# Four-layer kernel on Trainium2, Mamba part: a third buffer for GpSimd's products, one fp32 matrix buffer, and two operations moved from GpSimd to VectorE

## The chip, the cores and the metric

One core of one Trainium2 chip runs the whole program in one launch. The metric is device time in microseconds (us), the median of repeated executions. The profile comes from one more execution under the hardware profiler. Engines: PE is TensorE, with PEld for its weight loads; DVE is VectorE; ACT is ScalarE; POOL is GpSimd; SP is SyncE, which issues most DMAs here.

## The reference, cut to what matters

The program computes four residual layers over a sequence of 4096 tokens of width 256: linear attention, a feed-forward layer, two Mamba blocks, and a mixture of experts. The change touches the Mamba blocks only. Their reference, for each of the two layers:

```
xz = x_norm @ in_w.T ; xb, z = split(xz)            # 512 channels each
xb = silu(causal_conv4(xb) + cb)
delta, Bm, Cm = split(xb @ xp_w.T)                  # 16, 16, 16 values per token
delta = softplus(delta @ dtw.T + dtb)               # per channel and token
dA = exp(delta[..., None] * -exp(a_log))            # per channel, token, state n of 16
mi = delta[..., None] * Bm * xb[..., None]
step t:  v = 0.6 * v + mi_t ; h = dA_t * h + v ; y_t = sum over n of h * C_t
out = ((y + dp * xb) * silu(z)) @ ow.T
```

## The kernel before, in words

**Tiling.** `mamba_phase` runs once per layer. A layer is 16 chunks of 256 tokens (`NCM`, `CM`). Channels lie on the partitions in four groups m of 128 (`KI`). A chunk has 16 slots, one for each state n. Two chunks make one turn of a hardware loop (`Fori`), except the first two and the last two on GpSimd and TensorE.

**One slot.** TensorE makes v (`velocity`, L1298 and L1300: 32 bf16 matmuls). ScalarE makes dA (`decays`, L1149). VectorE runs four scans for h (`scan`, L1019). GpSimd multiplies h by the row C of this state (`product`, L898), into the fp32 tile `hc`. TensorE adds `hc` over the states with an identity matrix (`accumulate`, L1282, in two halves). The scans lie in a ring of four buffers, `hc` in two: product k waits until product k-2 is added (`acc_done`), and also until the first scan of slot n+1 is done. TensorE adds product n-2 in slot n, behind the velocity matmuls of slot n+1, half by half.

**Work of other chunks in the slots.** A slot has two steps, `at` = 2n and 2n+1. Beside the slot's own work each engine runs `tail(...)`, which ends the chunk before (the gate with skip and y, L1002 on VectorE; times silu(z), L888 on GpSimd; output projection L1271; its sum into the residual, L1008 on VectorE), and `head(c+1, ..., at+10)`, which prepares the next chunk. The order on each engine is written out by hand by these step numbers, and every engine works its list in order.

**The steps of `head` that matter here**, by their number (the slot is that number less 10, halved):

- 21: GpSimd makes `Gf` (L866) and the first matrix `Mf[:, 0]` (L843), decay times B. There are two, for the two halves of 128 tokens. 23: the second one.
- 22 to 26: softplus. ScalarE: L1109, exp L1115, square L1118, exp L1122, logarithm L1125. VectorE: clamp L975 at 23, the series L979 at 26.
- 24 and 27: ScalarE rounds `Mf` to bf16, `Mhi` (L1130). 25 and 30: GpSimd makes the rest, `Mlo` (L849).
- 27: VectorE ends delta with L984 and two L986. GpSimd: `Glo`, the low part of the matrix of the carries (L876).
- 28: GpSimd makes `u` = delta times xb (L880). 30: TensorE transposes it (L1247). 31 to 35: bf16 parts (L1135, L992), carries, and the DMAs that place the parts for the next chunk.

**Loops and queues.** SP places the bf16 matrices when both halves of `Mhi`, and then of `Mlo`, are there; it spreads the rows of C two states at a time behind the products. Neither list is changed.

Of the kernel before, what the change touches and what calls it, by code (L numbers as in the profile page):

```python
# [14 lines left out]
ALU = mybir.AluOpType  # L15
# [649 lines left out]
def mamba_phase(net, layer, xm):  # L665
# [4 lines left out]
    with ExitStack() as ctx:  # L670
# [16 lines left out]
        Mf = sb("Mf", [P, TM, NS, SUB])  # L687
# [10 lines left out]
        hc = sb("hc", [P, 2, KI, CM])  # L698
# [20 lines left out]
        with nc.Block() as block:  # L719
            @block.sync  # L720
            def _(sp):
# [7 lines left out]
                for part in range(3):  # L729
                    at = SUB + part * NS  # L730
                    sp.dma_start(Mf[at:at + NS, 0], dram["decay"][SUB:SUB + NS]).then_inc(s["loaded"], 16)
                    sp.dma_start(Gf[at:at + NS, 0], dram["carry_on"]).then_inc(s["loaded"], 16)
# [96 lines left out]
            def _(pool):  # L829
# [11 lines left out]
                def matrix(q, j):  # L841
                    pool.wait_ge(s["b_done"], 1 + q + 1)
                    nc.gpsimd.tensor_tensor(Mf[:, j], decay_n, Bs[:, j, :].unsqueeze(2).broadcast_to([P, NS, SUB]),  # L843
                                            ALU.mult).then_inc(s["mf_done"], 1)

                def matrix_low(q, j):
                    pool.wait_ge(s["mhi_done"], 1 + q * TM + j + 1)
                    pool.wait_ge(s["m_moved"], 1 + 6 * 16 * q)
                    nc.gpsimd.tensor_tensor(Mlo[:, j], Mf[:, j], Mhi[:, j], ALU.subtract).then_inc(s["mlo_done"], 1)  # L849

                def head(q, par, at):
# [18 lines left out]
                    if at == 23:  # L870
                        matrix(q, 1)
                    if at == 25:
                        matrix_low(q, 0)
                    if at == 27:
                        pool.wait_ge(s["ghi_done"], 1 + q + 1)
                        nc.gpsimd.tensor_tensor(Glo[:], Gf[:].rearrange("p j i n -> p j (i n)"), Ghi[:],  # L876
                                                ALU.subtract).then_inc(s["glo_done"], 1)
                    if at == 28:
                        pool.wait_ge(s["delta_done"], 1 + q + 1)
                        nc.gpsimd.tensor_tensor(u[:], delta[:, par], xb[:, par], ALU.mult).then_inc(s["u_done"], 1)  # L880
# [9 lines left out]
                def product(c, par, n, next_scan=1):  # L890
# [3 lines left out]
                    pool.wait_ge(s["acc_done"], 1 + AHEAD + k - 1)  # L894
# [3 lines left out]
                    nc.gpsimd.tensor_tensor(hc[:, n % 2], h[:, n % RING],  # L898
# [32 lines left out]
            def _(dve):  # L931
# [3 lines left out]
                for par in range(2):  # L935
                    nc.vector.memset(U2[SUB:KV, par, 0], 0.0)
                    for j in range(NSUB):
                        nc.vector.tensor_copy(M2[SUB:SUB + 2 * NS, par, j], Mf[SUB:SUB + 2 * NS, 0])
                        nc.vector.tensor_copy(M2[SUB + 2 * NS:KV, par, j], Mf[SUB + 2 * NS:KV, 0])
# [4 lines left out]
                for par in range(2):  # L944
                    for j in range(NSUB):
                        nc.vector.tensor_tensor(M2[SUB + 2 * NS:KV, par, j], Mf[SUB + 2 * NS:KV, 0],
# [14 lines left out]
                def head(q, par, at):  # L961
# [19 lines left out]
                    if at == 27:  # L981
# [6 lines left out]
                        last.then_inc(s["delta_done"], 1)  # L988
                    if at == 32:
# [60 lines left out]
            def _(act):  # L1050
# [13 lines left out]
                def head(q, par, at):  # L1064
# [61 lines left out]
                    if at in (24, 27):  # L1126
# [1060 lines left out]
```

## Time and profile before

| | |
|---|---|
| runs | 4496.07, 4501.99, 4504.96 us; median 4501.99 us |
| profiled execution | 4487.59 us, span of the trace 4485.9 us |
| mean granted TensorE clock | 0.866 of full speed |
| busy over the span | PE 79%, DVE 62%, POOL 46%, ACT 44% |
| first Mamba layer, first to last scan | 1058.8 to 2296.7 us |
| second Mamba layer | 2410.9 to 3658.5 us |

Busy shares are means over the whole program. PE is the busiest engine, but a share doesn't tell which wait ends last in a slot: for that the timeline of one chunk is needed, engine by engine, with the idle time ahead of each instruction in brackets.

### The profile page before, as it was taken

Reading aid. Unit: us, or ns where it says so; the run is one execution under the profiler, and the core shown is the slowest. Engines: PE = TensorE matmul, PEld = TensorE weight load, DVE = VectorE, ACT = ScalarE, POOL = GpSimd, SP = SyncE. Lnnn points to the kernel's source line nnn. Section 1 sums busy time; section 2 is a strip of 40 time slices with the busy share of each in tenths; the row PEclk is TensorE's granted clock in tenths of the full one; section 3 lists DMA queues with packets and bytes.
Section 4 is the critical chain, followed back from the end, with each engine's and each line's share of the span. In section 5 each row is a group of like instructions: output and inputs, shape, how many; then the busy total and the mean of one; then the engine's idle time right before and its main releaser. Section 6 shows DMA issues by size and latency. Waiting matters only on the chain. (4 is left out here: it accounts for less than half of the span.)

```text
span 4485.9 us, 88366 instructions
## 1 busy us (share of the span) xinstructions
PE 3543.9 (79%) x28412; PEld 2364.3 (53%) x28413; DVE 2774.5 (62%) x4814; ACT 1980.0 (44%) x4446; POOL 2046.1 (46%) x1206
## 2 busy tenths in 40 slices
PE   6888869936898888888856988889888863199980
PEld 4554546614555555555534555555555543188870
DVE  3444432345777777777765777777777767255545
ACT  1212112215666565665625666566565633133320
POOL 0101000014666676666744667676676764500006
PEclk8888878967999999999987999999999985599995
DMA  4000000012223121231211212122121223311113
GB/s 143 0 0 0 0 21 0 0 56 55 59 53 76 49 74 52 52 74 48 74 38 45 69 50 73 51 60 66 51 73 51 62 74 106 141 47 47 49 37 109
DMA packets 152098, 244.93 MB, mean 55 GB/s; under 512 B 25714, under 2 KB 74130, under 8 KB 149012
## 3 DMA queue, kind: packets, MB, share of 16 engines
q1 hardware_dynamic: 142356, 212.69, 17.4%
q0 software_dynamic: 9344, 27.27, 1.8%
q8 instruction: 208, 3.41, 0.3%
q14 instruction: 190, 1.56, 0.1%
HBM read 119.89 MB, written 38.27 MB: 35 GB/s over the span
## 5 line engine op out<-in xcount | busy, mean ns | idle before, releaser
L898 POOL TENSOR_TENSOR m_hc<-m_h,m_Cb 128x1024 f32<-128x1024 f32 x512 | 1205.4, 2355 | 763.5 <-DVE m_h L1019 466.2
L1019 DVE TENSOR_TENSOR_SCAN m_h<-m_dA,m_hlast,m_bank 128x256 f32<-128x256 f32 x2048 | 1354.2, 725 | 140.1 <-PE m_bank L1300 74.0
L1282 PE MATMUL m_bank<-m_hc,ident 128*128 128x512 f32 x2048 | 1207.7, 679 | 148.5 <-POOL m_hc L898 148.3
L1149 ACT ACTIVATE m_dA<-m_delta,m_rate 128x256 f32<-128x256 f32 x2048 | 894.1, 500 | 16.4 <-DVE m_h L1019 15.4
L1298 PEld LDWEIGHTS m_bank<-m_M,m_U 128*128 128x128 bf16 x8192 | 605.0, 101 | 358.3 <-DVE m_h L1019 222.2
L1298 PE MATMUL m_bank<-m_M,m_U 128*128 128x64 bf16 x8192 | 674.9, 197 | 124.5 <-DVE m_h L1019 117.0
L1300 PEld LDWEIGHTS m_bank<-m_M,m_U 112*128 112x128 bf16 x8192 | 578.5, 100 | 204.5 <-issue 172.6
L1300 PE MATMUL m_bank<-m_M,m_U 112*128 112x64 bf16 x8192 | 675.2, 197 | 0.0
L1282 PEld LDWEIGHTS m_bank<-m_hc,ident 128*128 128x128 f32 x2048 | 337.3, 204 | 198.0 <-POOL m_hc L898 164.9
L967 DVE SCALAR_TENSOR_TENSOR m_cv<-m_xpre,m_conv,m_cv 128x256 f32<-128x256 f32 x384 | 273.3, 753 | 22.6 <-ACT m_cv L1087 18.1
L1212 PE MATMUL m_bank<-m_pair,m_in 128*128 128x256 f32 x1024 | 268.7, 389 | 8.2 <-ACT m_cv L1087 4.4
L1947 ACT ACTIVATE x_h<-x_bank,x_b 128x256 f32<-128x256 f32 x320 | 134.4, 471 | 284.9 <-PE x_bank L1893 277.3
L1212 PEld LDWEIGHTS m_bank<-m_pair,m_in 128*128 128x128 f32 x1024 | 194.6, 194 | 120.0 <-issue 93.9
L108 POOL TENSOR_SCALAR var_eps<-a_mv 128x4 f32<-128x4 f32 x16 | 3.7, 229 | 524.8 <-DVE a_mv L120 524.8
L1861 POOL DMA_DIRECT2D slots_y<-x_y x40 | 21.7, 542 | 445.7 <-DVE x_y L1988 445.7
L403 PE MATMUL a_bank<-a_qh,a_phi 128*128 128x512 f32 x256 | 144.5, 699 | 48.1 <-DVE a_qh L238 39.0
L1893 PE MATMUL x_bank<-x_xhi,r_wlo 128*128 128x256 bf16 x640 | 175.8, 275 | 6.0 <-issue 5.0
L1893 PE MATMUL x_bank<-x_xlo,r_whi 128*128 128x256 bf16 x640 | 175.6, 274 | 0.0
L1893 PE MATMUL x_bank<-x_xhi,r_whi 128*128 128x256 bf16 x640 | 175.5, 274 | 0.0
L1906 PE MATMUL x_bank<-r_whi,x_hhi 128*128 x640 | 174.4, 273 | 0.0
L1906 PE MATMUL x_bank<-r_whi,x_hlo 128*128 x640 | 174.4, 273 | 0.0
L1906 PE MATMUL x_bank<-r_wlo,x_hhi 128*128 x640 | 174.4, 273 | 0.0
(260 smaller groups left out, 5594.2 us busy)
## 6 DMA issues: line engine op xcount, KB each, us to landing
m_Cb<-m_c_rows SPq DMA_DIRECT2D x256, 256.0 KB, 3.2
m_M<-m_Mhi SPq DMA_DIRECT2D x128, 256.0 KB, 4.1
m_M<-m_Mlo SPq DMA_DIRECT2D x64, 256.0 KB, 3.9
m_U<-m_Uhi SPq DMA_DIRECT2D x128, 128.0 KB, 3.3
slots_x<-x_res SPq DMA_DIRECT2D x40, 256.0 KB, 3.0
x_x_in<-slots_x SPq DMA_DIRECT2D x40, 256.0 KB, 2.6
slots_y<-x_y POOLq DMA_DIRECT2D x40, 256.0 KB, 2.3
m_U<-m_Ulo SPq DMA_DIRECT2D x64, 128.0 KB, 3.6
```

The source lines that it names most:

```text
L403: nc.tensor.matmul(B[5 + g % 2][:].rearrange("p (h t) -> p h t", h=4), phi[:, KD + g // 2, t], qh[:, 4 * g:4 * g + 4, t], start=True, stop ...
L898: nc.gpsimd.tensor_tensor(hc[:, n % 2], h[:, n % RING], Cb[:, g % 2, n % NG, :].unsqueeze(1).broadcast_to([P, KI, CM]), ALU.mult).then_inc ...
L967: i = nc.vector.scalar_tensor_tensor(cv[:, m, :], xpre[:, m, k:k + CM], conv[:, m, k:k + 1], cv[:, m, :], ALU.mult, ALU.add)
L1019: nc.vector.tensor_tensor_scan(h[:, n % RING, m, :], dA[:, n % RING, m, :], VB[(n % 2) * 2 + g][:, (m % 2) * CM:(m % 2 + 1) * CM], hlast[: ...
L1149: nc.scalar.activation(dA[:, n % RING, m, :], delta[:, par, m, :], ACT.Exp, scale=rate[:, m, n:n + 1]).then_inc(s["da_done"], 1)
L1212: last = nc.tensor.matmul((H0, H1)[g % 2][:, m % 2 * CM:(m % 2 + 1) * CM], w_in[:, k, m * P:(m + 1) * P], xT[:, k, :], start=(k == 0), sto ...
L1282: last = nc.tensor.matmul(Y[half][:], net.ident[:], hc[:, n % 2, 2 * half:2 * half + 2, :], start=(n == 0), stop=(n == NS - 1))
L1298: nc.tensor.matmul(bank[:, at:at + SUB], U1[:, par, j, m * P:(m + 1) * P], M1[:, par, j, n, :], start=True, stop=False)
L1300: last = nc.tensor.matmul(bank[:, at:at + SUB], U2[:, par, j, m * P:(m + 1) * P], M2[:, par, j, n, :], start=False, stop=True)
L1893: last = nc.tensor.matmul(out, w_part[:, bass.ts(e * WB + kk * KH + m, P)], x_part[:, par, kk, :], start=(kk == 0 and n == 0), stop=(kk == ...
L1906: last = nc.tensor.matmul(YB[par][:, t * D:(t + 1) * D], h_part[:, par, m, t * P:(t + 1) * P], w_part[:, bass.ts(e * (WB // 2) + KD * KH / ...
L1947: last = nc.scalar.activation(h[:, g % 2, m % 2, :], HB[g][:, m % 2 * SLOT:(m % 2 + 1) * SLOT], ACT.Relu, bias=b1[:, bass.ts(e[par] * KH + ...
```

## The change

`hc` gets three buffers; product and accumulation take buffer (n + par) mod 3, where par is the chunk's parity. Product k then waits until product k-3 is added; across the chunks' border, where the numbers jump, two products keep the shorter distance. `Mf` has one buffer for both halves, so the second matrix is made behind `Mlo` of the first. `u` and `Glo` go to VectorE, `u` right behind delta, `Glo` at step 29. `Mhi` of the first half moves from 24 to 23 on ScalarE.

```diff
-        Mf = sb("Mf", [P, TM, NS, SUB])
+        Mf = sb("Mf", [P, NS, SUB])
-        hc = sb("hc", [P, 2, KI, CM])
+        hc = sb("hc", [P, 3, KI, CM])
...
                 def matrix(q, j):
                     pool.wait_ge(s["b_done"], 1 + q + 1)
+                    pool.wait_ge(s["mlo_done"], 1 + q * TM + j)
...
                         matrix(q, 0)
-                    if at == 23:
+                    if at == 24:
+                        matrix_low(q, 0)
+                    if at == 25:
+                        pool.wait_ge(s["mlo_done"], 1 + q * TM + 1)
                         matrix(q, 1)
-                    if at == 25:
-                        matrix_low(q, 0)
-                    if at == 27:
-                        pool.wait_ge(s["ghi_done"], 1 + q + 1)
-                        nc.gpsimd.tensor_tensor(Glo[:], Gf[:]..., Ghi[:], ALU.subtract)
-                    if at == 28:
-                        pool.wait_ge(s["delta_done"], 1 + q + 1)
-                        nc.gpsimd.tensor_tensor(u[:], delta[:, par], xb[:, par], ALU.mult)
                     if at == 30:
                         matrix_low(q, 1)
...
-                    pool.wait_ge(s["acc_done"], 1 + AHEAD + k - 1)
+                    pool.wait_ge(s["acc_done"], 1 + AHEAD + k - (1 if par == 0 and n < 2 else 2))
-                    nc.gpsimd.tensor_tensor(hc[:, n % 2], h[:, n % RING],
+                    nc.gpsimd.tensor_tensor(hc[:, (n + par) % 3], h[:, n % RING],
...
                         last.then_inc(s["delta_done"], 1)          # VectorE, step 27
+                        dve.wait_ge(s["delta_done"], 1 + q + 1)
+                        nc.vector.tensor_tensor(u[:], delta[:, par], xb[:, par], ALU.mult)
+                    if at == 29:
+                        dve.wait_ge(s["ghi_done"], 1 + q + 1)
+                        nc.vector.tensor_tensor(Glo[:], Gf[:]..., Ghi[:], ALU.subtract)
...
-                    if at in (24, 27):
-                        j = (at - 24) // 3
+                    if at in (23, 27):
+                        j = (at - 23) // 4
                         act.wait_ge(s["mf_done"], 1 + q * TM + j + 1)
-                        nc.scalar.copy(Mhi[:, j], Mf[:, j])
+                        nc.scalar.copy(Mhi[:, j], Mf[:])
```

The accumulation on TensorE takes its buffer by the same rule.

## Rows read from the trace of the kernel before

**Rows 1.** Windows: us; each engine's busy us (instructions); clock, DMA share, GB/s.
```profile
1058.80:2296.70 1237.90, 1095.04 (x10459) 687.32 (x10459) 952.96 (x1419) 768.32 (x1792) 842.82 (x418) 0.93 0.23 60
1824.50:1830.00 5.50, 5.18 (x27) 3.15 (x27) 4.20 (x8) 2.11 (x5) 5.50 (x3) 0.50 0.61 149
```

**Rows 2.** Waits, 1290 to 2168 (11 chunks): who for whom, us, times, longest.
```profile
PE m_bank L1282 <- POOL m_hc L898: 51.3, 33, 2.2
PE m_bank L1298 <- DVE m_h L1019: 40.4, 21, 2.7
PE m_bank L1247 <- POOL m_u L880: 8.3, 11, 1.3
...
POOL m_hc L898 <- PE m_bank L1282: 88.4, 56, 4.1
```

**Rows 3.** Timeline of VectorE, tenth chunk of layer 0: start, us, instruction, [idle before].
```profile
1808.76 3.93 DVE L1019 TENSOR_TENSOR_SCAN m_h<-m_dA,m_hlast,m_bank 128x256 f32<-128x256 f32 x6
1812.61 1.39 DVE L979 SCALAR_TENSOR_TENSOR m_pair<-m_pair,m_cv 128x1024 f32<-128x1024 f32 x1
...
1817.30 2.08 DVE L984 SCALAR_TENSOR_TENSOR m_u<-m_u,m_floor,m_pair 128x1024 f32<-128x1024 f32 x1 [2.01 <-ACT m_u L1125]
1819.41 1.29 DVE L986 TENSOR_TENSOR m_delta<-m_bank,m_u 128x512 f32<-128x512 f32 x2
1820.62 6.48 DVE L1019 TENSOR_TENSOR_SCAN m_h<-m_dA,m_hlast,m_bank 128x256 f32<-128x256 f32 x10
```

**Rows 4.** Timeline of GpSimd in the same stretch.
```profile
1808.69 1.90 POOL L843 TENSOR_TENSOR m_Mf<-m_decay,m_Bs 128x1024 f32<-128x1024 f32 x1
1810.55 2.37 POOL L898 TENSOR_TENSOR m_hc<-m_h,m_Cb 128x1024 f32<-128x1024 f32 x1
1812.87 3.11 POOL L849 TENSOR_TENSOR m_Mlo<-m_Mf,m_Mhi 128x1024 bf16<-128x1024 f32 x1
1815.95 2.34 POOL L898 TENSOR_TENSOR m_hc<-m_h,m_Cb 128x1024 f32<-128x1024 f32 x1
1818.25 1.41 POOL L876 TENSOR_TENSOR m_Glo<-m_Gf,m_Ghi 128x128 bf16<-128x128 f32 x1
1821.70 2.35 POOL L898 TENSOR_TENSOR m_hc<-m_h,m_Cb 128x1024 f32<-128x1024 f32 x1 [2.04 <-DVE m_h L1019]
1824.01 2.35 POOL L880 TENSOR_TENSOR m_u<-m_delta,m_xb 128x1024 f32<-128x1024 f32 x1
```

**Rows 5.** Timeline of ScalarE in the same stretch.
```profile
1811.21 1.04 ACT L1130 CAST m_Mhi<-m_Mf 128x1024 bf16<-128x1024 f32 x1
...
1816.21 1.06 ACT L1125 ACTIVATE m_u<-m_u 128x1024 f32<-128x1024 f32 x1
```

**Rows 6.** Timeline of TensorE in the same stretch.
```profile
1824.11 2.08 PE L1282 MATMUL m_bank<-m_hc,ident 128*128 128x512 f32 x2 [1.38 <-POOL m_hc L898]
1826.50 1.94 PE L1247 MATMUL m_bank<-ident,m_u 128*128 128x128 f32 x8 [0.32 <-POOL m_u L880]
```

**Rows 7.** One line each: count, shortest/median/longest ns, first and last start.
```profile
L984 DVE SCALAR_TENSOR_TENSOR m_u<-m_u,m_floor,m_pair x32: 1283/2078/2547, 1033.7 to 3575.4; 128x1024 f32<-128x1024 f32 x32
...
L849 POOL TENSOR_TENSOR m_Mlo<-m_Mf,m_Mhi x64: 2118/2190/3180, 1030.5 to 3586.4; 128x1024 bf16<-128x1024 f32 x64
...
L298 DVE TENSOR_TENSOR x_res<-x_res,a_zn x8: 1224/1225/1227, 112.9 to 647.4; 128x1024 f32 x7, 128x1024 f32<-128x1024 f32 x1
```

**Rows 8.** Timeline of VectorE and GpSimd at the start of that chunk.
```profile
1771.90 4.56 DVE L967 SCALAR_TENSOR_TENSOR m_cv<-m_xpre,m_conv,m_cv 128x256 f32<-128x256 f32 x6
1779.24 1.66 DVE L1002 SCALAR_TENSOR_TENSOR m_u<-m_xb,m_skip,m_bank 128x256 f32<-128x256 f32 x4 [0.20 <-PE m_bank L1282]
...
1771.60 2.36 POOL L898 TENSOR_TENSOR m_hc<-m_h,m_Cb 128x1024 f32<-128x1024 f32 x1 [2.23 <-PE m_bank L1282]
```

**Rows 9.** Timeline of VectorE and GpSimd at the end of layer 0.
```profile
2294.00 2.67 DVE L1019 TENSOR_TENSOR_SCAN m_h<-m_dA,m_hlast,m_bank 128x256 f32<-128x256 f32 x4 [0.23 <-PE m_bank L1300]
...
2296.35 4.64 POOL L898 TENSOR_TENSOR m_hc<-m_h,m_Cb 128x1024 f32<-128x1024 f32 x2 [0.53 <-PE m_bank L1282]
```

More of the change, by code:

```diff
@@ L848, in matrix_low @@
                     pool.wait_ge(s["m_moved"], 1 + 6 * 16 * q)
-                    nc.gpsimd.tensor_tensor(Mlo[:, j], Mf[:, j], Mhi[:, j], ALU.subtract).then_inc(s["mlo_done"], 1)
+                    nc.gpsimd.tensor_tensor(Mlo[:, j], Mf[:], Mhi[:, j], ALU.subtract).then_inc(s["mlo_done"], 1)
                 def head(q, par, at):
@@ L937, in _ @@
                     for j in range(NSUB):
[L938 to L939 removed]
+                        nc.vector.tensor_copy(M2[SUB:SUB + 2 * NS, par, j], Mf[SUB:SUB + 2 * NS])
+                        nc.vector.tensor_copy(M2[SUB + 2 * NS:KV, par, j], Mf[SUB + 2 * NS:KV])
                 on = Gf[:, 0].rearrange("p i n -> p (i n)")
@@ L988, in head @@
                         last.then_inc(s["delta_done"], 1)
+                        dve.wait_ge(s["delta_done"], 1 + q + 1)
+                        nc.vector.tensor_tensor(u[:], delta[:, par], xb[:, par], ALU.mult).then_inc(s["u_done"], 1)
+                    if at == 29:
+                        dve.wait_ge(s["ghi_done"], 1 + q + 1)
+                        nc.vector.tensor_tensor(Glo[:], Gf[:].rearrange("p j i n -> p j (i n)"), Ghi[:],
+                                                ALU.subtract).then_inc(s["glo_done"], 1)
                     if at == 32:
@@ L1274, in tail, with accumulate @@
                             last.then_inc(s["out_psum"], 1)
-                def accumulate(c, n, half):
+                def accumulate(c, par, n, half):
                     k = c * NS + n
@@ L1281, in accumulate @@
                         pe.wait_ge(s["gate_done"], 1 + c * KI + 2 * half + 2)
-                    last = nc.tensor.matmul(Y[half][:], net.ident[:], hc[:, n % 2, 2 * half:2 * half + 2, :],
+                    last = nc.tensor.matmul(Y[half][:], net.ident[:], hc[:, (n + par) % 3, 2 * half:2 * half + 2, :],
                                             start=(n == 0), stop=(n == NS - 1))
@@ L1302, in velocity, with late @@
                     last.then_inc(s["v_psum"], 1)
-                def late(c, n, half):
+                def late(c, par, n, half):
                     if not (isinstance(c, int) and c == 0):
-                        accumulate(c - 1, n + NS - 2, half)
+                        accumulate(c - 1, 1 - par, n + NS - 2, half)
                 def slots(c, par, more, more2):
@@ L1345, in _ @@
                 for n in range(2):
-                    late(NCM, n, 0)
-                    late(NCM, n, 1)
+                    late(NCM, 0, n, 0)
+                    late(NCM, 0, n, 1)
                 tail(NCM, 1, 7, False)
```

23 lines of the change are left out of this document (10 added, 13 removed).

## The prediction

> **What bounds the kernel now.** The change touches only the two Mamba layers, so I went from the page's shares to windows over one layer, then to the waits by pair, then to the timeline of one chunk, engine by engine. The window over the first layer lasts 1237.9 us; PE is busy in 1095.0 of them (88%), DVE in 953.0, POOL in 842.8 [rows 1]. For 16 chunks that is 77 us a chunk. No engine is full, but PE is close: its idle time is small and sits in a few places. The waits say which: over 11 chunks PE waits 51.3 us for GpSimd's products, 40.4 us for scans, 8.3 us for u [rows 2], so 9.1 us a chunk in the first two. GpSimd in turn waits 88.4 us, 8.0 a chunk, for the accumulations of the buffer that it wants to write [rows 2]; this is what a third buffer can remove. The reader is to ask of each of these waits whether something later depends on it.
>
> The timeline of a chunk answers. Of the 33 waits for products in 11 chunks three fall in each chunk, for products 1, 7 and 8 [rows 2]; from 1826.5 (slot 10) until the gate of the next chunk (L1002) PE has none. A product that comes earlier there finds PE with other work ahead of it. The gate itself waits 0.20 us for PE [rows 8], so PE also sets it. PE does wait in slots 8 to 10. There the order is: softplus on ScalarE ends at 1816.21 + 1.06 = 1817.27 [rows 5]; L984 on VectorE starts at 1817.30 but takes 2.08 us, where its shortest is 1.28 [rows 3, 7]. It ends at 1819.38, which is 1.09 after product 7 on GpSimd ended (1815.95 + 2.34 = 1818.29) [rows 4]. So L984, with two inputs in SBUF, did not run while the product ran. The same shows the other way round: the first Mlo takes 3.11 instead of its shortest 2.12 [rows 4, 7], being held until L979 ended at 1814.00; and L979 took 1.39 since it was held until product 6 ended at 1812.92, then needed 1.08. Behind L984 come two L986 (1.29), then scan 9 at 1820.62 [rows 3], product 8 at 1821.70 (1.08 after the scan's start), its addition on PE at 1824.11, and the transposes at 1826.50 [rows 4, 6]. This chain, ACT and POOL, then DVE, POOL, PE, sets the chunk's time.
>
> **The change part by part.**
>
> *One Mf buffer.* Before, the second Mf (1.90) filled the time ahead of product 6. Now product 6 follows product 5 and has to wait for the first scan of slot 7: 1808.76 + 1.08 (the same distance as at product 8) = 1809.84, so 0.71 earlier than 1810.55. It ends at 1812.2, and Mlo starts there; Mhi is ready, since ScalarE makes it one step earlier. L979 comes at 1812.61 [rows 3], finds Mlo running and is held until 1812.16 + 2.12 = 1814.28, then takes 1.08: 1815.36. The second Mf has to wait for Mlo's completion, so L979 gets in first; Mf then needs 1.90 less the 0.14 of its start that lies under the wait (the held Mlo ran 1.98 behind L979, against 2.12): 1817.12. Product 7 starts at 1817.1, where it started at 1815.95 [rows 4]. L984 still comes at 1817.30, because ScalarE's list has the same work in another order (Mhi's 1.04 moves ahead of the square, which then ends where Mhi ended, at 1812.25 at the latest [rows 5], still ahead of L979). Product 7 is 0.2 us ahead of L984. It runs to 1819.44, and L984 ends 1.08 later, at 1820.52, instead of 1819.38: **+1.14**.
>
> *u on VectorE.* It stands directly ahead of scan 9. Its price is that of a fp32 multiplication or addition of 1024 elements with both inputs in SBUF: L298, 1.225 us in all eight cases [rows 7]. Bounds: 1.08 (what L984 needs once it is let in) and 1.225 + 2.35, if a product is running in front of it. I take 1.225, less nothing, since after 1821.84 GpSimd is idle until scan 9. Scan 9 comes at 1820.62 + 1.14 + 1.24 = 1823.00: **+2.38**, and so do product 8 and its addition. What is saved is u on GpSimd (2.35), which was late for the transposes by 0.32 only [rows 6]: at 1824.11 + 2.38 the addition starts, 2.07 later the transposes, which wait for nothing now: 1828.57 against 1826.50. **+2.07 a chunk.** From there PE is full up to the gate, so it hands the delay on unchanged.
>
> *Glo on VectorE.* On GpSimd it took 1.41, nearly all of it held by L984 [rows 4]. On VectorE it stands behind scan 9's second half and has to wait until product 8 ends, at most 2.35. It must be there for the carries some 9 us later, and VectorE stands idle before L992 anyway. At nothing; if that cover goes, up to 0.9 for scan 10, between zero and that; I take zero.
>
> *The third buffer.* It removes most of the 8.0 us a chunk for which GpSimd waits for PE. None of the products that PE waits for (1, 7, 8) waits for an accumulation: they start behind scans or back to back. At nothing in 30 chunks; bounds -1.4 (below) and 0. At the end of a layer it counts: the last two products run back to back from 2296.35 [rows 9], and product 14 could have started at 2294.00 + 1.08 = 2295.1, so product 15 ends 1.3 us sooner: -1.3 for each layer, -2.6 in all. In each layer's first, unoverlapped head u costs 1.2 less, but the later Mf and Mlo stand in front of L984 and of u; I take zero, between -1.2 and +1.2.
>
> *TensorE's clock.* Behind its idle time PE runs at 0.50 of its clock, 1.2 GHz, from 1824.5 to 1830 [rows 1], and ahead of that it waited for products 7 and 8 and a scan [rows 2, 6]. The additions are at the low level there before and after; I add nothing. Idle time grows by 2 us, so if it falls sooner, an addition more is slow; it takes 2.08 at this level [rows 6], so +1 at the most.
>
> *Sum.* 15 chunks of 16 in each layer carry a head: 30 × 2.07 = +62, less 2.6: **+59 us**. On the profiled execution, 4487.6, that is 4547; on the median of the runs, 4502.0 (0.3% above the profiled one), 4561.
>
> A rule of the Trainium skill bears on the sum. The page "SBUF — State Buffer", section "SBUF: two separate sides", says that VectorE and GpSimd share one pair of ports as an exclusive lock, which a VectorE instruction with two SBUF inputs needs, and that the first to start keeps it to its end. The trace agrees for L984 and L979; no row of it shows a TENSOR_TENSOR of VectorE beside a GpSimd operation. If the pair were shared by bandwidth, the one Mf buffer would cost nothing and only u would count. The page "GPSIMD Engine Reference", section "Engine selection", advises VectorE for two-input elementwise work, as GpSimd takes about twice the time; the rows agree (2.35 against 1.225), and by that rule alone the change would gain, since it frees 2.35 + 1.41 of GpSimd for 1.4 of VectorE. I hold it for misleading here, because GpSimd's u lay beside PE's addition and VectorE's lies in the chain.
>
> **Rivals.**
>
> *B, L984 comes first.* The 0.2 us between product 7 and L984 is thin. If L984 is let in at 1817.30, it ends at 1818.58, L986 at 1819.9; product 7 ends at 1818.58 + 2.2 = 1820.8; u is held by it and ends 1.08 later, 1821.9. Scan 9 is then +1.2, the transposes +0.87: 30 × 0.87 - 2.6 = +23, 4525. For it: a delay of GpSimd's dispatch of 0.2. Against: back to back operations there show no gap [rows 4].
>
> *C, the delay is absorbed.* Somewhere between slot 10 and the next slot 8 a wait shrinks by what was added: no change, 4502. Against it: PE's list is full up to the gate, and from the gate on the chain runs through DVE, POOL and PE again.
>
> *D, faster.* The first convolution of a chunk (L967, six) takes 4.56 us, because product 15 holds it from 1771.90 to 1771.60 + 2.36 = 1773.96 [rows 8]: 2.06 lost, and with the third buffer product 15 is out of the way by then. If the gate depended on VectorE, this would come back; I take 1.5 as the mean of a chunk, between none and 2.06, so 45 us; with B's +23 that gives -22, 4480. It decides from the point where VectorE reaches the gate later than PE. Against: the gate waits for PE, by 0.20 even in this chunk [rows 8].
>
> *E, it doesn't do what it says.* A product still waits for its buffer, as the distance at the chunks' border stays short: it would take away the -2.6 only.
>
> **How the numbers follow.** Forecast (E with it) 0.55, own range 4549 to 4571 (the clock's and Glo's bounds above, the ends' below); B 0.23; C 0.10; D 0.12. The range holds forecast and B with what lies between and some above: 4508 to 4574. About 9 us, 0.2%, is what a measurement of this kernel can tell. Slower 0.55 + 0.23 = 0.78, same 0.10, faster 0.12.
>
> **What would show it.** Product 6 about 1.1 us behind the first scan of slot 7, L979 near 2.8 us long, product 7 starting ahead of L984, and L984 near 3.2 us long: the step of the one buffer. L984 near 1.3 and u near 2.2: B. u 1.2 us on VectorE and then scan 9: the second step. Products 12 to 15 without waits for PE, PE's waits unchanged: the third buffer off the path. Wrong would be transposes less than 18 us behind the first scan of slot 7 (17.7 before, 19.8 by the forecast, 18.6 by B), or a gate that no longer waits for PE.

## The result, and the profile after

| | before | after |
|---|---|---|
| median of 13 runs each, on the same chips | 4490.92 us (4480.94 to 4504.96) | 4525.75 us (4506.19 to 4536.18) |
| ratio | | 1.0078, 95% interval 1.0064 to 1.0091 |
| profiled execution | 4487.59 us, clock 0.866 | 4533.29 us, clock 0.864 |
| both Mamba layers, first to last scan | 2485.5 us | 2533.0 us |

Slower, as forecast, by 34.8 us (0.78%) where 59 (1.3%) was forecast. The forecast's base, 4502, was 11 us too high as well: it was a median of three runs. All the time is in the two Mamba layers, which are 47.5 us longer in the profiled executions. The whole profiled executions differ by 45.7 us; they lie 3 us below and 8 us above their medians, which makes up the difference to 34.8.

The windows over both layers (columns as in [rows 1]), after:

```profile
1059.51:2321.29 1261.78, 1101.07 (x10466) 695.15 (x10463) 996.27 (x1449) 769.30 (x1792) 787.01 (x388) 0.92 0.23 59
2435.20:3706.45 1271.25, 1108.55 (x10464) 698.92 (x10461) 997.10 (x1449) 768.90 (x1792) 786.87 (x388) 0.92 0.23 58
```

GpSimd is relieved: 787.0 us busy where it was 842.8 [rows 1]. VectorE has 43 more. TensorE does the same work and waits longer. The waits after, in the same stretch of time as in [rows 2], 10.8 chunks now:

```profile
POOL m_hc L893 <- DVE m_h L1020: 254.5, 102, 9.3
PE m_bank L1283 <- POOL m_hc L893: 63.5, 33, 3.3
PE m_bank L1299 <- DVE m_h L1020: 43.4, 22, 2.7
POOL m_hc L893 <- PE m_bank L1283: 40.9, 5, 8.2
```

GpSimd's waits for additions went from 56 to 5, and what it waits for now is scans. The five are product 0 of every second chunk, at the border where the distance stayed short. TensorE's waits for products are 33 as before, and grew from 51.3 to 63.5 [rows 2]: the third buffer removed waits for which nothing was late. The growth is at product 7, for which TensorE waits 3.26 us in the mean of a chunk and waited 2.18 before. The wait for u is gone.

The tenth chunk of layer 0 again, VectorE and then GpSimd, as [rows 3, 4]. The first scan of slot 7 is at 1820.83 (1808.76 before). Line numbers have shifted: the series is L974 here (L979 before), and the line with two inputs that ends softplus is L979 here (L984 before). That one is called "the last softplus step" below. The accumulation, L1283 here, is called the addition.

```profile
1820.83 3.93 DVE L1020 TENSOR_TENSOR_SCAN m_h<-m_dA,m_hlast,m_bank 128x256 f32<-128x256 f32 x6
1824.67 2.72 DVE L974 SCALAR_TENSOR_TENSOR m_pair<-m_pair,m_cv 128x1024 f32<-128x1024 f32 x1
...
1829.36 3.17 DVE L979 SCALAR_TENSOR_TENSOR m_u<-m_u,m_floor,m_pair 128x1024 f32<-128x1024 f32 x1 [0.67 <-ACT m_u L1126]
1832.57 1.29 DVE L981 TENSOR_TENSOR m_delta<-m_bank,m_u 128x512 f32<-128x512 f32 x2
1833.89 1.23 DVE L985 TENSOR_TENSOR m_u<-m_delta,m_xb 128x1024 f32<-128x1024 f32 x1
1835.04 2.65 DVE L1020 TENSOR_TENSOR_SCAN m_h<-m_dA,m_hlast,m_bank 128x256 f32<-128x256 f32 x4
1837.60 1.01 DVE L988 TENSOR_TENSOR m_Glo<-m_Gf,m_Ghi 128x128 bf16<-128x128 f32 x1
```

```profile
1821.85 2.37 POOL L893 TENSOR_TENSOR m_hc<-m_h,m_Cb 128x1024 f32<-128x1024 f32 x1 [1.04 <-DVE m_h L1020]
1824.18 2.12 POOL L850 TENSOR_TENSOR m_Mlo<-m_Mf,m_Mhi 128x1024 bf16<-128x1024 f32 x1
1826.48 2.67 POOL L844 TENSOR_TENSOR m_Mf<-m_decay,m_Bs 128x1024 f32<-128x1024 f32 x1 [0.17 <-POOL m_Mlo L850]
1829.12 2.34 POOL L893 TENSOR_TENSOR m_hc<-m_h,m_Cb 128x1024 f32<-128x1024 f32 x1
1836.12 2.35 POOL L893 TENSOR_TENSOR m_hc<-m_h,m_Cb 128x1024 f32<-128x1024 f32 x1 [4.67 <-DVE m_h L1020]
```

Up to scan 9 every step follows the forecast: product 6 is 1.02 behind the scan (1.08), Mlo follows it, the series is held and takes 2.72 (2.75), the second Mf comes next, product 7 starts at 1829.12, which is 0.24 ahead of the last softplus step, and that takes 3.17 (3.22), up to 1.1 behind product 7's end. u takes 1.23. Scan 9 is 14.21 behind slot 7's first scan, where 14.24 was forecast and 11.86 was before.

On TensorE, the addition of product 8 and the transposes:

```profile
1838.52 2.07 PE L1283 MATMUL m_bank<-m_hc,ident 128*128 128x512 f32 x2 [1.37 <-POOL m_hc L893]
1840.39 0.85 PE L1248 MATMUL m_bank<-ident,m_u 128*128 128x128 f32 x3
```

The transposes start 19.56 behind slot 7's first scan, against 17.74 before: +1.82 in this chunk, where the forecast had +2.07. They start 1.87 behind the start of the addition, although its record is 2.07 long. Over the 28 chunks that are neither the first nor the last of a layer the means are: scan 9 from 11.89 to 14.19 (+2.30), transposes from 17.76 to 19.41 (+1.65), whole chunk from 79.59 to 81.14 (+1.55). So the delay shrinks between scan 9 and the transposes, and in this execution little of it is lost behind them.

### The profile page after: what moved, and what is told of

The parts are those of the page before. It is cut to its first block and busy times, and to the rows that moved or that the text cites. A ratio compares the mean times of both kernels' runs of the same rounds, so it can differ in the third digit from the quotient of the medians.

```text
span 4531.6 us, 88430 instructions
## 1 busy us (share of the span) xinstructions
PE 3560.8 (79%) x28412; PEld 2383.5 (53%) x28413; DVE 2864.7 (63%) x4878; ACT 1980.8 (44%) x4446; POOL 1927.6 (43%) x1142
## 5 line engine op out<-in xcount | busy, mean ns | idle before, releaser
L1283 PE MATMUL m_bank<-m_hc,ident 128*128 128x512 f32 x2048 | 1220.1, 685 | 176.8 <-POOL m_hc L893 176.4
L1283 PEld LDWEIGHTS m_bank<-m_hc,ident 128*128 128x128 f32 x2048 | 340.6, 206 | 225.0 <-POOL m_hc L893 191.1
L962 DVE SCALAR_TENSOR_TENSOR m_cv<-m_xpre,m_conv,m_cv 128x256 f32<-128x256 f32 x384 | 230.7, 643 | 24.6 <-ACT m_cv L1088 20.0
L1009 DVE TENSOR_TENSOR x_res<-x_res,m_bank 128x512 f32 (+1 forms) x34 | 23.4, 688 | 248.8 <-PE m_bank L1272 248.8
```

Of the source, the lines that this page charges most:

```text
L962: i = nc.vector.scalar_tensor_tensor(cv[:, m, :], xpre[:, m, k:k + CM], conv[:, m, k:k + 1], cv[:, m, :], ALU.mult, ALU.add)
L1283: last = nc.tensor.matmul(Y[half][:], net.ident[:], hc[:, (n + par) % 3, 2 * half:2 * half + 2, :], start=(n == 0), stop=(n == NS - 1))
```

## The experiments

"Milestones" are means over those 28 chunks of one profiled execution: scan 9 and the transposes in us behind the first scan of slot 7, and the length of the chunk, from its first scan to the next chunk's first scan. "Half-clock time" is the sum of all stretches in the two layers for which the trace has TensorE at 1.2 GHz.

| kernel | time to before | 95% interval | scan 9 | transposes | chunk | half-clock time |
|---|---|---|---|---|---|---|
| before | 1 | | 11.89 | 17.76 | 79.59 | 358 |
| after | 1.0078 | 1.0064 to 1.0091 | 14.19 | 19.41 | 81.14 | 406 |
| only_mf | 0.9986 | 0.9974 to 0.9999 | 11.37 | 18.24 | 79.25 | 338 |
| only_u | 1.0013 | 1.0001 to 1.0024 | 13.09 | 18.43 | 79.87 | 410 |
| only_glo | 0.9998 | 0.9988 to 1.0008 | 11.83 | 17.75 | 79.78 | 372 |
| after_hc2 | 1.0015 | 1.0005 to 1.0025 | 13.35 | 18.45 | 79.64 | 358 |
| flip | 1.0017 | 1.0006 to 1.0028 | 13.25 | 18.04 | 79.97 | 355 |
| after_u_pool | 1.0055 | 1.0037 to 1.0073 | 12.93 | 18.84 | 80.49 | 324 |
| flip_u_pool | 0.9999 | 0.9989 to 1.0008 | 11.45 | 18.12 | 79.71 | 352 |
| dose2 | 1.0121 | 1.0105 to 1.0137 | 14.35 | 19.68 | 81.20 | 420 |
| dose3 | 1.0203 | 1.0189 to 1.0216 | 15.61 | 20.94 | 82.53 | 437 |
| late_mf | 1.0401 | 1.0376 to 1.0426 | 12.35 | 17.68 | 85.80 | 502 |
| late_both | 1.0403 | 1.0379 to 1.0426 | 11.09 | 16.01 | 85.65 | 495 |
| late_mf_sp | 1.0135 | 1.0117 to 1.0153 | 12.35 | 17.68 | 81.69 | 375 |
| warm_after | 1.0090 | 1.0071 to 1.0110 | 14.20 | 19.41 | 80.96 | 389 |

### The parts one by one

The third buffer was not tried alone, beside two Mf; it was left out of the changed kernel instead. **only_mf** is before with one Mf buffer and its order, nothing else; **only_u** and **only_glo** move one operation; **after_hc2** is after with two buffers of products.

```diff
only_mf (to before; also the rest of the change's lines for Mf)
-        Mf = sb("Mf", [P, TM, NS, SUB])
+        Mf = sb("Mf", [P, NS, SUB])
-                    if at == 23:
+                    if at == 24:
+                        matrix_low(q, 0)
+                    if at == 25:
+                        pool.wait_ge(s["mlo_done"], 1 + q * TM + 1)
                         matrix(q, 1)
-                    if at == 25:
-                        matrix_low(q, 0)
-                    if at in (24, 27):                # ScalarE
+                    if at in (23, 27):
...
only_glo (to before)
-                    if at == 27:                      # GpSimd
+                    if at == 29:                      # VectorE
                         Glo = Gf - Ghi                # in words
...
only_u (to before)
-                    if at == 28:                      # GpSimd
-                        nc.gpsimd.tensor_tensor(u[:], delta[:, par], xb[:, par], ALU.mult)
                         last.then_inc(s["delta_done"], 1)
+                        dve.wait_ge(s["delta_done"], 1 + q + 1)
+                        nc.vector.tensor_tensor(u[:], delta[:, par], xb[:, par], ALU.mult)
...
after_hc2 (to after)
-        hc = sb("hc", [P, 3, KI, CM])
+        hc = sb("hc", [P, 2, KI, CM])
-                    pool.wait_ge(s["acc_done"], 1 + AHEAD + k - (1 if par == 0 and n < 2 else 2))
+                    pool.wait_ge(s["acc_done"], 1 + AHEAD + k - 1)
-                    nc.gpsimd.tensor_tensor(hc[:, (n + par) % 3], h[:, n % RING],
+                    nc.gpsimd.tensor_tensor(hc[:, n % 2], h[:, n % RING],
...
```

> The kernel before with the single Mf buffer and its order on GpSimd and ScalarE alone (Mlo of the first half at step 24, second Mf at 25, Mhi at 23); hc keeps two buffers, u and Glo stay on GpSimd. All theories: product 7 starts about 8.3 us behind the first scan of slot 7 (7.2 before), L979 about 2.7 us long, L984 about 3.2, scan 9 at +1.1, the transposes at +1.1. Theory 1 (TensorE's half-clock stretch slides into its longer idle time, so only part of the delay reaches the next chunk): +5 to +20 us. Theory 2 (the delay is handed on whole, as forecast): 30 x 1.1 = +34 us. Theory 3 (this part is harmless, the multiplication on VectorE is what costs): within 5 us.

> The kernel before with u on VectorE right behind delta and nothing else. All theories: product 7 and L984 as before (L984 about 2.08 us), u about 1.22 us, scan 9 at +1.24, the transposes at +0.9 or less. Theory 1 (the half-clock stretch absorbs a part): +3 to +15 us. Theory 2 (handed on whole): 30 x 0.92 = +28 us. Theory 3 (this multiplication is what costs): all of the +35 us.

> The kernel before with Glo on VectorE at step 29 and nothing else. Glo on VectorE stands behind scan 9 and may be held by product 8, by up to 0.9 us; before it was held by L984 on GpSimd and cost the chain nothing. Theories 1 and 2: within 6 us of before. Rival (the hold in front of scan 10 counts): 30 x 0.9 = +27 us.

> The changed kernel with hc back at two buffers, all else as changed. Theory 1 and 2 (the third buffer lies off the path but for the layers' ends): 2 to 3 us slower than the changed kernel, so about +38 us on the kernel before, with GpSimd's waits for L1283 back at 7 to 8 us a chunk. Rival: the third buffer hides a part of the cost, since the product 15 of a chunk then no longer holds the first convolution: 10 us or more slower than the changed kernel, +45 us or more.

Measured: 4485.5, 4496.4, 4489.4 and 4496.1 us against 4491.0. No part alone costs what the whole does, and the changed kernel without its third buffer costs 5 us in place of 35. only_mf is not slower at all, though it was the part to which the forecast gave +1.14. Its VectorE and GpSimd in the same chunk show why:

```profile
1808.81 3.93 DVE L1021 TENSOR_TENSOR_SCAN m_h<-m_dA,m_hlast,m_bank 128x256 f32<-128x256 f32 x6
...
1817.34 1.28 DVE L986 SCALAR_TENSOR_TENSOR m_u<-m_u,m_floor,m_pair 128x1024 f32<-128x1024 f32 x1 [0.36 <-ACT m_u L1127]
1818.66 1.29 DVE L988 TENSOR_TENSOR m_delta<-m_bank,m_u 128x512 f32<-128x512 f32 x2
1819.87 3.93 DVE L1021 TENSOR_TENSOR_SCAN m_h<-m_dA,m_hlast,m_bank 128x256 f32<-128x256 f32 x6
```

```profile
1810.14 2.37 POOL L900 TENSOR_TENSOR m_hc<-m_h,m_Cb 128x1024 f32<-128x1024 f32 x1 [1.37 <-PE m_bank L1284]
...
1814.78 2.67 POOL L844 TENSOR_TENSOR m_Mf<-m_decay,m_Bs 128x1024 f32<-128x1024 f32 x1 [0.17 <-POOL m_Mlo L850]
1817.41 3.44 POOL L900 TENSOR_TENSOR m_hc<-m_h,m_Cb 128x1024 f32<-128x1024 f32 x1
```

With two buffers product 6 waits for TensorE (1.37), not for the scan: it starts 1.33 behind slot 7's first scan and not 1.02. Product 7 is then 0.07 behind the last softplus step and is the one that is held (3.44), while the softplus step takes 1.28. That is rival B. The forecast had product 6 wait for the scan alone, which is true only with the third buffer; costed "at nothing", it is what decides the race between product 7 and the last softplus step, that is, which of the two starts first and holds the other.

### The race alone: flip, and with u on GpSimd after_u_pool and flip_u_pool

**flip** is after with one number changed: product 6 alone keeps the shorter distance. **after_u_pool** is after with u back on GpSimd at step 28 (the diff leaves out the waits); **flip_u_pool** has both edits.

```diff
flip (to after)
-                    pool.wait_ge(s["acc_done"], 1 + AHEAD + k - (1 if par == 0 and n < 2 else 2))
+                    pool.wait_ge(s["acc_done"], 1 + AHEAD + k - (1 if par == 0 and n < 2 or n == 6 else 2))
after_u_pool (to after)
-                        nc.vector.tensor_tensor(u[:], delta[:, par], xb[:, par], ALU.mult)   # behind delta
+                    if at == 28:
+                        nc.gpsimd.tensor_tensor(u[:], delta[:, par], xb[:, par], ALU.mult)
```

> The changed kernel, three buffers and all, with one number altered: product 6 alone waits again until product 4 is added, as with two buffers. Theory 4 (the third buffer costs by winning a race: it lets product 6 start 0.3 us earlier, 1.02 in place of 1.33 us behind the first scan of slot 7, so that product 7 comes 0.26 us ahead of L984 instead of 0.06 behind it): product 6 at 1.33, L984 near 1.3 us long in most chunks, scan 9 at about 13.1 instead of 14.2, and 20 to 35 us faster than the changed kernel, at +0.1 to +0.3% of before. Rival (the third buffer costs in another way, by its place in memory or by the earlier products at the chunk's end, which this leaves alone): within 8 us of the changed kernel.

> The changed kernel with u back on GpSimd at step 28: third buffer, one Mf and Glo on VectorE stay. Product 7 is still ahead of L984 (8.28 against 8.54), L984 ends at 11.70, scan 9 comes at 12.97 (+1.1 on before), product 8 at 14.05 to 16.40, u on GpSimd to 18.75, transposes at 18.8 (+1.1). Theory K goes by scan 9: within the free part, +5, 1.001, 4496. Rival, the forecast's rule that what the transposes lose is handed on: 30 x 1.1 = +33, 1.0073, 4524.

> The changed kernel with u on GpSimd and product 6 waiting for product 4's addition (0.3 us later, so that L984 is ahead of product 7): it differs from the kernel that lost 25 us with u on GpSimd in this one number. If the race alone costs those 25 us, scan 9 comes at 11.1 (12.93 there), the transposes near 18.2 or earlier (18.84), and the time is that of the kernel with one Mf alone: 4485 to 4492, 0.9986 to 1.0005. Rival: the third buffer costs by itself (later products, other DMA times): 4505 or more, 1.004.

Measured: 4497.8 against 4491.5; 4515.0 against 4489.4; 4495.6 against 4495.6. In flip the same chunk reads (VectorE, then GpSimd):

```profile
1810.29 3.93 DVE L1020 TENSOR_TENSOR_SCAN m_h<-m_dA,m_hlast,m_bank 128x256 f32<-128x256 f32 x6
...
1818.82 1.28 DVE L979 SCALAR_TENSOR_TENSOR m_u<-m_u,m_floor,m_pair 128x1024 f32<-128x1024 f32 x1 [0.37 <-ACT m_u L1126]
1820.14 1.29 DVE L981 TENSOR_TENSOR m_delta<-m_bank,m_u 128x512 f32<-128x512 f32 x2
1821.46 1.94 DVE L985 TENSOR_TENSOR m_u<-m_delta,m_xb 128x1024 f32<-128x1024 f32 x1
```

```profile
1811.62 2.37 POOL L893 TENSOR_TENSOR m_hc<-m_h,m_Cb 128x1024 f32<-128x1024 f32 x1 [1.36 <-PE m_bank L1283]
...
1818.88 3.44 POOL L893 TENSOR_TENSOR m_hc<-m_h,m_Cb 128x1024 f32<-128x1024 f32 x1
```

The four kernels with one Mf, three buffers and Glo on VectorE make a square:

| | product 7 ahead | softplus step ahead | the race costs |
|---|---|---|---|
| u on GpSimd | 1.0055 | 0.9999 | 0.56%, 25 us |
| u on VectorE | 1.0078 | 1.0017 | 0.61%, 27 us |
| u on VectorE costs | 0.23%, 10 us | 0.18%, 8 us | |

The race costs 25 to 27 us and u 8 to 10 us. That the two add up to 35 along either way is how a square is made; what it finds is that its fourth corner, with the race won and u on GpSimd, is at 0.9999, and that each price is nearly the same in both rows. Going by the intervals of the corners, the race's price is known to about 9 us, and u's is only just clear of zero. Beyond the race the third buffer costs nothing that these runs can tell: flip has it and is at 1.0017, after_hc2 has not and is at 1.0015.

In flip u takes 1.94 and ends 1.08 behind product 7; so a TENSOR_TENSOR of VectorE with two inputs in SBUF is held as well. No row of before showed this: the two L986 that run beside Glo in [rows 3, 4] have one input in PSUM.

### How much of a delay is handed on: dose2, dose3

Before, with u on VectorE made twice and three times in a row; `after(...)` has VectorE wait for the end of one before the next. The diff is to only_u.

```diff
+                        after(nc.vector.tensor_tensor(u[:], delta[:, par], xb[:, par], ALU.mult))   # 1 or 2 times more
                         nc.vector.tensor_tensor(u[:], delta[:, par], xb[:, par], ALU.mult)
```

> The kernel before, with u made on VectorE twice in a row (the second overwrites the first with the same values) ahead of scan 9; the race for the port and the buffers stay as before. It delays scan 9 by about as much as the whole change does, without the third buffer: 11.85 + 2.5 = 14.35 us behind the first scan of slot 7 (14.20 in the changed kernel, 13.11 with one u). Theory K (what the change costs hangs on when scan 9 comes, and the first 1.2 us of delay are nearly free): as slow as the changed kernel, 1.0078, 4526. Rival L (the price grows in proportion, 5.5 us for 1.25, and the third buffer costs something in another place): +11, 1.0025, 4502. The forecast's own passing-on (all of the delay of the transposes, 0.74 + 1.25) would give +60, 1.013.

> The same with u made three times: scan 9 at about 15.6, 3.7 us later than before. Theory K: behind the free part each us of delay costs 30 us, so 35 + 30 x 1.25 = +72, 1.016, 4563; if TensorE's half-clock time takes up a share of it, +60, 1.013. Rival L: +17, 1.004, 4508.

Measured: 4542.0 and 4579.1 against 4489.4. In dose2:

```profile
1837.51 1.23 DVE L987 TENSOR_TENSOR m_u<-m_delta,m_xb 128x1024 f32<-128x1024 f32 x1
1838.77 1.23 DVE L988 TENSOR_TENSOR m_u<-m_delta,m_xb 128x1024 f32<-128x1024 f32 x1
1839.91 6.48 DVE L1019 TENSOR_TENSOR_SCAN m_h<-m_dA,m_hlast,m_bank 128x256 f32<-128x256 f32 x10
```

From one u to two to three, the scan moves by 1.26 each time, the transposes by 1.25 and 1.26, and the chunk by 1.33 both times; the times of the runs by 47 and 37 us (30 × 1.26 = 38), the layers of the profiled executions by 40 and 36. So the forecast's rule, that TensorE hands the transposes' delay on unchanged, nearly holds from there on. Only the first u is cheap: scan 9 +1.20, transposes +0.67, chunk +0.28, runs +5.4. Both theories of these expectations fell: L at once, and K, since after_u_pool pays 25 us for a scan 9 that comes 1.04 later, where it should have been free. What a kernel loses goes with the transposes and not with scan 9: after_hc2 and flip have scan 9 at +1.46 and +1.36 and lose 5 and 6 us, after_u_pool has it at +1.04 and loses 25; their transposes are at +0.69, +0.28 and +1.08. But there is no fixed sum to take off. The chunk is longer by the transposes' delay less 0.82 in only_mf, 0.64 in after_hc2, 0.39 in only_u and 0.10 in after, and by 0.10 more than it in flip.

### Where TensorE's clock comes in: warm_after, look_a, look_b

**warm_after** writes the first half of slot 10's velocity matmuls four times, to keep TensorE busy there. **look_a** and **look_b** are the changed kernel, profiled again.

```diff
warm_after (to after)
-                    for m in (2 * g, 2 * g + 1):
+                    for m in (2 * g, 2 * g + 1) * (4 if (n, g) == (10, 0) else 1):
```

> The changed kernel with the 16 velocity matmuls of slot 10's first half written four times over (1.6 us more work for TensorE in each chunk, at a place where it would wait 3.3 us for product 7; the extra ones write the same values). Theory 5 (part of the cost of a longer wait is that TensorE's clock falls to half in it, for a stretch in which the additions and transposes run): the half-clock time a chunk falls by 3 us or more and the kernel is 10 to 40 us faster than the changed one in spite of the added work. Rival (the clock is a by-product): within 8 us of the changed kernel, or slower.

> The changed kernel, unchanged, profiled once more. In its first profiled execution (4533) the two layers are 47.5 longer than before, 1.55 a chunk; its 13 runs spread from 4506 to 4536 around 4526. Theory P (the size depends on where the half-clock stretches fall): the same times up to scan 9 in every chunk, 14.2 behind the first scan of slot 7, but the distance from there to the transposes and from these to the chunk's end varies, and a faster execution has less half-clock time than 406 us. Rival S: the times from scan 9 to the end are the same too, and an execution near 4515 is faster outside the Mamba layers.

> A second such look at the changed kernel, with the same expectations: theory P, scan 9 at 14.2 throughout, and the whole time follows the half-clock time in the Mamba layers, about half a microsecond for each; rival S, the layers as long as in the first, to within 3 us.

Measured: warm_after 4530.7 against 4491.5, no gain. Half-clock time was 389 us, which lies inside the 372 to 406 of the changed kernel's own executions below, so the edit did not bring about what it was to test, and the theory is neither confirmed nor refuted by it. look_a and look_b took 4538.1 and 4507.7 us. Their windows over the layers, look_a first, look_b second:

```profile
1060.24:2326.26 1266.02, 1104.66 (x10476) 697.85 (x10473) 996.41 (x1449) 769.15 (x1792) 786.46 (x388) 0.92 0.23 58
2440.69:3708.63 1267.94, 1103.61 (x10459) 695.88 (x10458) 996.73 (x1449) 769.11 (x1792) 786.38 (x388) 0.92 0.23 58
```

```profile
1051.00:2302.07 1251.07, 1095.43 (x10470) 691.59 (x10467) 995.24 (x1449) 769.25 (x1792) 786.55 (x388) 0.93 0.23 59
2412.82:3678.40 1265.58, 1104.26 (x10471) 696.32 (x10468) 996.38 (x1449) 769.33 (x1792) 786.39 (x388) 0.92 0.23 58
```

| changed kernel | layers | half-clock time | scan 9 | transposes | chunk |
|---|---|---|---|---|---|
| first profile | 2533.0 | 406 | 14.19 | 19.41 | 81.14 |
| look_a | 2534.0 | 403 | 14.19 | 19.39 | 81.05 |
| look_b | 2516.7 | 372 | 14.19 | 19.34 | 80.54 |

Theory P holds: the mean of scan 9 is the same to 0.01 in all three, and the layers differ by 16.4 us for 34 us of half-clock time between the first and look_b, which is about half a microsecond for each. The Trainium skill, "TensorE: Matmul & The Clock Gate", section "Terms", gives the penalty as the time at the reduced clock times one minus its ratio, here one half. By that rule the 34 us are worth 17, and for this pair the traces agree. The layers' excess over before is 47.5, 48.5 and 31.2 us in three executions of one kernel, so one profiled execution is not the median: the 35 of the runs is inside this spread. With half of the extra half-clock time taken off, 24, 26 and 24 us are left. That is steady within this kernel, but no split that holds between kernels: the same subtraction leaves -16 us of only_u's +9.9. Nor is the clock the race's price: after_u_pool has the least half-clock time of all, 324 us, and is 25 us slower than before.

Where a delay shrinks or grows behind the transposes shows when the chunk is cut in two there (means over the same 28 chunks, us, with the half-clock time in brackets):

| | transposes to the next chunk's first scan | TensorE idle in it | first scan to slot 7's first scan |
|---|---|---|---|
| before | 21.18 (3.67) | 0.07 | 40.65 (4.75) |
| only_u | 20.83 (3.05) | 0.02 | 40.61 (4.88) |
| after | 20.54 (2.47) | 0.08 | 41.20 (5.49) |
| look_b | 20.52 (2.29) | 0.08 | 40.68 (4.51) |

In the first stretch TensorE has the same work and next to no idle time, and still it is 0.64 us shorter in after, with 1.20 us less at half clock, and 0.35 shorter in only_u, with 0.62 less. So a full TensorE does not hand a delay on whole: where the transposes start later, less of what follows them runs at half clock, and about half a microsecond comes back for each one less. The second stretch takes it away again in part, or not: +0.55 us in the first profile of after, with 0.74 us more at half clock, and +0.03 in look_b, with 0.24 less. What sets the half-clock time of one execution stays open.

### A later second Mf: late_mf, late_both, late_mf_sp

A try to keep the third buffer and get product 7 out of the way: the second Mf moved behind product 8 (step 28), its Mhi to 29; **late_both** also puts u at 29 and Glo at 31; **late_mf_sp** is late_mf with one line moved on SyncE.

```diff
late_mf (to after)
-                    if at == 25:                      # GpSimd, second Mf
+                    if at == 28:
-                    if at in (23, 27):                # ScalarE, Mhi
+                    if at in (23, 29):
late_both (to late_mf, VectorE)
+                    if at == 29:
                         nc.vector.tensor_tensor(u[:], delta[:, par], xb[:, par], ALU.mult)
-                    if at == 29:
+                    if at == 31:                      # Glo
...
late_mf_sp (to late_mf, SyncE)
-                    if not last:
-                        place_high(c + 1, 1 - par)
                     spread(c, par, 5)
+                    if not last:
+                        place_high(c + 1, 1 - par)
```

> The changed kernel with the second Mf behind product 8 (step 28) and its Mhi at step 29. Product 7 then follows Mlo and L979 and ends at about 8.8 us behind the first scan of slot 7, so it holds L984 (8.54) for 0.3 us only. Theory 4: L984 about 1.6 us, scan 9 at about 12.4 (11.86 before, 14.2 changed), 25 to 45 us faster than the changed kernel. Rival (as for flip): within 8 us of the changed kernel. The second Mf stands in front of product 9, which may then come up to 0.5 us later than before.

> late_mf with u on VectorE at step 29, behind scan 9, and Glo at 31. Theory 4 with the chain as read: scan 9 at about 11.2, product 8 at 12.3, the transposes at 15.7 to 16.7 (17.7 before): 10 to 40 us faster than before. Rival (u is held by product 8 and moves scan 10 back by 1.5 us, which the chain pays): no faster than late_mf.

> The kernel with the second Mf at step 28, which lost 4%, with one line moved on SyncE: the DMAs of Mhi are issued behind the sixth spread of C rows, not ahead of it. Theory: the 4% came from that queue alone (product 10 waited for C rows that stood behind SyncE's wait for the second Mhi), so it comes back to the kernels where L984 is ahead of product 7: scan 9 at 12.35, 4485 to 4500, 0.999 to 1.002. Rival: the late second Mhi itself, or its DMAs beside the next work, costs: over 1.02.

Measured: 4666.7 and 4667.7 against 4491.5, 4549.6 against 4489.4. Scan 9 and the transposes come where they were expected, at 12.35 in late_mf and at 11.09 and 16.01 in late_both, and the time does not follow: the transposes of late_mf are 1.73 earlier than in after, and its chunks are 4.7 us longer all the same. The loss lies later in the chunk, in GpSimd's products and in the queue of SyncE (late_mf, GpSimd, then SyncE):

```profile
1881.32 2.12 POOL L850 TENSOR_TENSOR m_Mlo<-m_Mf,m_Mhi 128x1024 bf16<-128x1024 f32 x1
1890.49 2.34 POOL L893 TENSOR_TENSOR m_hc<-m_h,m_Cb 128x1024 f32<-128x1024 f32 x1 [7.05 <-issue]
```

```profile
1861.34 0.32 SPq L741 DMA_DIRECT2D m_Cb<-m_c_rows  x1
1880.14 3.47 SPq L751 DMA_DIRECT2D m_M<-m_Mhi  x4
1883.74 1.09 SPq L741 DMA_DIRECT2D m_Cb<-m_c_rows  x1
```

SyncE works its list in order. The rows of C for product 10 stand behind the four DMAs of Mhi, which now wait for the second Mf: GpSimd stands idle for 7.05 us ahead of product 10. In its waits over the same stretch of time, some 10 chunks here, that is

```profile
POOL m_hc L893 <- issue: 70.4, 17, 7.0
```

With the two exchanged, in late_mf_sp:

```profile
POOL m_hc L893 <- issue: 3.8, 8, 1.6
PE m_bank L1299 <- DMA m_U<-m_clo: 15.5, 10, 2.5
DVE m_h L1020 <- PE m_bank L1301: 52.4, 40, 3.9
```

The 70.4 us are 3.8, and two thirds of the loss come back (1.0401 to 1.0135), less than expected (0.999 to 1.002), and below the rival's 1.02 as well. What remains shows in new waits at the next chunk's start: TensorE waits for the carries' DMA ten times in some 10.7 chunks, 1.55 us on average, and VectorE for velocities 52.4 us, where it was 18.1 in after. The late Mhi on ScalarE stands ahead of the work that makes the carries; that this is the rest is argued from the order of the list and was not tried.

## Why the prediction was right in sign and wrong in size

- **One Mf buffer, +1.14 on the last softplus step.** Right in place, mechanism and size: product 7 ahead by 0.24 (0.2), the step 3.17 us long (3.22). The race costs 25 to 27 us in the runs; 30 × 1.14 = 34 was the forecast. The attribution was wrong: with one Mf buffer alone the race is lost in 6 chunks of 30 only, and nothing is lost in time (0.9986). It takes the third buffer to start product 6 by 0.3 earlier.
- **The third buffer "at nothing in 30 chunks".** Wrong. The forecast looked for waits of TensorE that it would remove, and rightly found none; it did not look at what an earlier product would collide with. It even timed product 6 as if no addition held it. These two errors cancel in the forecast of the whole, which is luck; for either part alone the forecast fails, as only_mf and after_hc2 show.
- **u on VectorE, +1.24 at scan 9.** Right: +1.20 alone, 1.26 from after_u_pool to after.
- **What u on GpSimd had cost: 0.32.** This is the first step that failed. The forecast put the transposes 2.07 behind the addition's start, by the length of its record, and so took only the 0.32 of idle time behind it for saved. Measured in the same chunk, the transposes start 1.87 behind it, since the next matmul's record begins 0.2 ahead of the addition's recorded end. The trace of before shows this too: in twelve places a matmul that waits for nothing starts 1.86 or 1.87 behind the start of a half-clock addition whose record is 2.07 or 2.08 long. Before, the transposes started 2.40 behind the addition in every chunk, as they waited for u; after, they start 1.75 behind it in the mean of 28 chunks, as the clock rises during the addition in 8 of them. So u had cost 0.53 at half clock and 0.65 in the mean. The forecast's +2.07 loses about 0.20 by the record's length, 0.12 by the clock and 0.08 at scan 9 (+2.30 in the mean, not +2.38), and the three profiles have +1.65, +1.62 and +1.58. 30 × 0.42 = 13 us of the miss.
- **"PE is full up to the gate, so it hands the delay on unchanged".** This is the second step that failed. TensorE is full there, but the same work takes 20.54 us in place of 21.18, as 1.20 us less of it runs at half clock. The chunk is longer by 1.55, 1.46 and 0.95 us in the three profiles, and by 34.8 / 30 = 1.16 going by the medians. In dose2 and dose3 every further 1.26 became 1.33; of a first, small delay 0.4 is lost (only_u).
- **TensorE's clock, "I add nothing".** Mis-sized. Half-clock time in the layers went from 358 to 406, 403 and 372 us, worth 24, 22 and 7 us at one half of it each. That is inside the forecast's bound of 1 us a chunk, and it differs by 17 us between executions of one kernel, more than the 11 us that divide the profiled executions' move (46) from the medians' (35).
- **Glo at nothing.** Right: 0.9998.
- **Rivals.** B, the softplus step first, is what happens with two buffers or a product 6 that is 0.3 us later; its price was too high (+23 forecast, 6.4 us measured in flip). C came true in part: after_hc2, only_u and the changed kernel lose a part of the delay behind the transposes. D's release happened and its gain did not: VectorE spends 43 us less on the convolutions of both layers, but the gate still waits for TensorE in 11 of 11 chunks, 25.6 us in all (11.5 before). E holds for product 0 of every second chunk, which waits for its buffer up to 8.8 us; no addition waits for that product, so it costs nothing that the trace shows.

So of the 24 us between the two moves, 59 and 35, some 13 are delay that the transposes never had, most of it by what u on GpSimd had cost. The other 11 are delay of the transposes that does not reach the chunk's end. The first profiled execution alone does not show them, the medians do, and they lie within what the half-clock time makes of one kernel.

## What to carry to other kernels

A buffer that removes a wait "that nobody is late for" still starts its work earlier: ask what that work meets, down to tenths of a microsecond where two engines hold each other, since the one that is first holds the other to its end (product 7 held the last softplus step in all 30 chunks of after). What a removed wait saves is not the idle time in its bracket: take the distance from start to start at a place of the same trace where nothing waits (1.87 us here, where the record said 2.07). A full engine with two clocks does not hand a delay on unchanged, so profile a kernel more than once before its excess is explained. When a step is moved, look at every in-order queue that waits for it: a DMA list that waits for a late tile holds back whatever stands behind it.

The best version found, only_mf at 0.9986 (0.9974 to 0.9999), is one matrix buffer with two product buffers and u on GpSimd: about 6 us faster than before, and the 4 KB of SBUF a partition are free. The interval only just leaves out 1, and it is the best of fourteen kernels, so the gain is not certain.

## What the runs showed that was not expected

- The race is decided within 0.03 us or so. In the four kernels where product 7 starts just behind the last softplus step (only_mf, after_hc2, flip, flip_u_pool: 120 chunks), the softplus step runs first in 93 of 96 chunks where the product is 0.05 to 0.07 behind, and in none of 24 where it is 0.015 to 0.035 behind: there the product runs in its 2.34 us and the softplus step is held (3.4 us), though its start is recorded first. That is the case in the first two chunks and the fifteenth of a layer, six times in each kernel. The three others that went the same way had the product 0.05 behind. In after_hc2 scan 9 comes at 13.04 or 14.5 by that. In after, with product 7 at least 0.24 ahead, all 30 are lost.
- Mf, whose record starts while the series runs on VectorE, takes 2.67, and 1.90 where nothing holds it.
- The changed kernel's 13 runs spread over 30 us. The distance from slot 7's first scan to scan 9 has the same mean to 0.01 us in its three profiled executions, while the half-clock time differs by 34 us. Over the 13 runs the time goes with the mean granted clock: 0.868 to 0.870 in the three fastest, 0.861 to 0.864 in the six slowest. That the half-clock stretches make the whole spread is likely and not shown.
